# Four-layer attention and feed-forward stack on one core: rounding, dequantising and values moved from VectorE to GpSimd, with a new order table

## Chip, core and metric

The kernel runs on one core of a Trainium2 chip. The metric is the device time of one execution in microseconds (us). A core has five engines that each work through their own list of instructions in order and meet only at semaphores: TensorE (PE in the rows, its weight loads apart as PEld), VectorE (DVE), ScalarE (ACT), GpSimd (POOL) and SyncE (SP), which here issues nearly all DMAs. Matmul results land in eight PSUM banks, which GpSimd does not read in this kernel.

## What is computed

A batch of 8 sequences of 256 tokens with 256 features passes through four layers. Each layer is a cross-attention with 16 heads of 16 features, followed by a different feed-forward part. The layers are numbered 0 to 3 in the code. What matters here is layer 2 and layer 3:

```python
# layer 2 attention: the values are normed, scaled and shifted (vn_scale, vn_bias)
value = _layernorm(kv @ Wv + bv, vn_scale, vn_bias)
# layer 2 feed-forward ("the wide layer": 256 -> 1024 -> 256)
def _act_quant(x):
    scale = 127.0 / jnp.clip(jnp.max(jnp.abs(x), axis=-1, keepdims=True), 1e-05)
    xq = jnp.clip(jnp.round(x * scale), -128.0, 127.0) / scale
    return x + jax.lax.stop_gradient(xq - x)
gate = jax.nn.silu(_bitlinear(x, w_gate)); up = _bitlinear(x, w_up)
return _bitlinear(gate * up, w_down)
# layer 3 attention: the values are the context itself, no projection
vh = v.reshape(B, S, H, D)
# layer 3 feed-forward: six 256 x 256 matrices of 4-bit numbers, dequantised, plus a low-rank part
w = q.astype(jnp.float32) / 7.5 - 1.0
w = w * jnp.repeat(scale, GROUP, axis=1)
base = jnp.einsum('btd,od->bto', x, w) + bias
lora = jnp.einsum('btr,or->bto', jnp.einsum('btd,rd->btr', x, la), lb)
```

Layers 0 and 1 have ordinary attention with a causal mask, then a sign-weight matmul (layer 0) and a mixture of 16 routed and 2 shared experts (layer 1).

## The kernel before

A batch element is one tile of 256 tokens, held as two row blocks of 128 tokens (`SJ = 2`), so the wide layer has 16 row blocks, numbered `T`. Each attention item `(L, b)` has 16 heads. Scores are computed twice: once for the row maxima (`maxima` on PE, `reduce` on DVE, L2196 in the causal layers and L2200 in the others), once transposed for the exponents (`score` on PE, `exp` on ACT, L1945). `values` multiplies by the values held in `v` (PE, L1637). Two halves of `v` serve successive items in turn: who writes values for an item must wait until the item two places earlier has finished its `values` (the semaphore `pv_done`).

All the work is written as small steps (a method of `Part` on each engine). Steps that belong together form a lane, a Python generator that yields between steps. The order in which the lanes advance is the long table `AT`, one row of numbers per lane: all numbers are sorted and the lane that owns the next number advances by one step. Every engine walks the same sorted list and emits only its own methods, so this table fixes the order of instructions on every engine and also the choice of PSUM banks. The numbers are sort keys, and nothing here reads them as times.

The items run in the order of `ORDER`: layers 0 and 1 interleaved first, then layer 2 with layer 3 four items behind. In the trace, layer 2's first exponents begin near 528 us and the last item, (3, 7), begins its exponents near 1094 us.

Steps of VectorE that the change touches, with their lines in the profile:

- `quantise(b)`: maximum of each row, scales (L2388 to L2396), then for each of two row blocks a multiply and round (L2401), and a subtract, clip and cast to bf16 into `xq` (L2408). PE transposes `xq` next (`quantised`, L1756).
- `hidden_quant(T)`: the same for 1024 features: maximum and scales (L2426 to L2431), round (L2433, 128 x 1024), clip and cast into `hid_q`, a part of `xn_t` (L2437). PE transposes it next (`down_turn`, L1778).
- `value_scale(b)`: multiply the normed values by a vector (L2176), then add one into `v` for each row block (L2181).
- `v_take(3, b)`: for layer 3, copy the context into `v` (L2161, two copies).
- `lora_add(n)`, six times: integers to f32 (L2374), times the group scales (L2378), plus the low-rank product from PSUM (L2381).

GpSimd has the small operations of every layer norm (`power`, L2517 to L2523: two tensor-scalar operations, a power, a multiply; ACT cannot norm before them), the lower parts of the split keys and queries (`split_low`, L2542 and L2544), bias additions (L2595, L2715), routing arithmetic, and indirect DMAs (L2681, L2694).

The lines around the value steps before:

```python
def value_scale(b):
    dve.wait_ge(*ln_done.at(("v", b, SJ - 1)))
    V.tensor_tensor(toks["v"], toks["v"], spread(V_L2VS, SJ), ALU.mult).then_inc(*tok_made.step(b))
    before = same_side_before(2, b)
    dve.wait_ge(*pv_done.at((*before, HG - 1)))
```

## Time and profile before

| | us |
|---|---|
| median of 3 runs | 1198.68 |
| lowest and highest | 1193.59, 1200.58 |
| the profiled execution, whole | 1198.55 |
| its span in the trace | 1196.6 |

The span is what the profile's rows cover, from the first to the last instruction. It is 1.95 us shorter than the profiled execution's own time, and that execution lies 0.13 us below the median. Busy times are sums over an engine's instructions. An engine's share of a stretch is its busy time divided by the length of the stretch. Matmul ends are modelled, so PE's share is to be read against other stretches of the same trace and not against 100%.

### The profile page before, as it was taken

The page shows a single profiled execution, that of the slowest core. Times are in us where ns is not written, and L with a number is a line of the kernel's source. Part 1 is how long each engine was busy: PE and PEld are TensorE (multiplying, and loading weights), DVE is VectorE, ACT ScalarE, POOL GpSimd, SP SyncE. Part 2 cuts the span into 40 slices and gives each one's busy share as a digit, 9 for nine tenths or more (in the row PEclk, how much of TensorE's full clock was granted, in tenths as well). Part 3 has the DMA queues.
Part 4 walks back from the last instruction along what each step waited for, and adds up shares of the span by engine and source line. Part 5 has one row for each costly group of instructions (what it writes and reads, how often), then busy time and mean ns, then how long its engine had stood idle before and what let it go on. Part 6 is the DMA issues. An engine that isn't in the chain of part 4 may idle for free.

```text
span 1196.6 us, 26279 instructions
## 1 busy us (share of the span) xinstructions
PE 1067.9 (89%) x8350; PEld 796.2 (67%) x8406; DVE 945.9 (79%) x3207; ACT 826.6 (69%) x1560; POOL 488.3 (41%) x1027
## 2 busy tenths in 40 slices
PE   6998999999999988899999988798899999988876
PEld 4676777777887765666677765366576766656654
DVE  3898888878555788877967798999999989898732
ACT  5777666657665666365667667457889798979953
POOL 6233356653122457657601144233334433423334
PEclk9999999999999999888999998999999999999988
DMA  7885332226777245303587752222203212121000
GB/s 221 260 275 180 87 101 71 85 76 189 218 211 213 89 121 140 85 14 116 150 259 229 233 167 80 56 69 82 82 19 87 72 54 81 53 63 54 10 10 18
DMA packets 102326, 140.03 MB, mean 117 GB/s; under 512 B 12336, under 2 KB 79792, under 8 KB 102192
## 3 DMA queue, kind: packets, MB, share of 16 engines
q1 hardware_dynamic: 99120, 129.97, 37.3%
q0 software_dynamic: 3072, 8.39, 2.2%
q8 instruction: 70, 1.15, 0.4%
q14 instruction: 64, 0.52, 0.1%
HBM read 65.43 MB, written 22.54 MB: 74 GB/s over the span
## 4 chain that ended last, share of the span: by engine, by line
PE 48%; DVE 20%; ACT 11%; DMA 7%; issue 6%; POOL 4%; SPq 3%; another core or an unknown queue 0%; DVEq 0%; ACTq 0%; POOLq 0%
PE ps L1516 10%; PE ps L1637 5%; PE ps L1536 4%; PE ps L1554 4%; PE ps L1729 4%; PE ps L1509 3%; DVE neg_max L2200 3%; PE ps L1523 3%; DVE ps L2196 3%; ACT probs L1945 3%; PE ps L1696 2%; DMA w<-in_expert 2%; ACT q_st L1960 2%; PE ps L1736 2%; DVE bn L2077 2%
## 5 line engine op out<-in xcount | busy, mean ns | idle before, releaser
L1945 ACT ACTIVATE probs<-ps 128x384 f32<-128x384 f32 (+1 forms) x512 | 263.5, 543 | 68.0 <-PE ps L1557 32.3
L1536 PE MATMUL ps<-k_st,q_st 96*128 96x256 bf16 (+1 forms) x1024 | 178.8, 265 | 19.4 <-DVE neg_max L2196 9.7
L1554 PE MATMUL ps<-q_st,k_st 104*128 104x256 bf16 (+1 forms) x1024 | 179.2, 263 | 14.8 <-ACT q_st L1960 6.7
L2200 DVE TENSOR_REDUCE neg_max<-ps 128x2 f32<-128x512 f32 x256 | 168.0, 679 | 11.7 <-PE ps L1536 4.9
L1960 ACT ACTIVATE q_st<-ps 8x1024 bf16<-8x1024 f32 x128 | 130.1, 1016 | 42.3 <-PE ps L1619 39.4
L2517 POOL TENSOR_SCALAR var_eps<-mv 128x2 f32<-128x2 f32 (+1 forms) x115 | 29.0, 252 | 298.0 <-DVE mv L2080 286.9
L2196 DVE CUSTOM_DVE_ANT_0 ps<-ps,diag_s 128x128 f32<-128x128 f32 (+1 forms) x384 | 123.3, 357 | 24.1 <-PE ps L1536 23.4
L1536 PEld LDWEIGHTS ps<-k_st,q_st 96*128 96x128 bf16 x1024 | 88.4, 100 | 70.3 <-DVE neg_max L2196 17.5
L1554 PEld LDWEIGHTS ps<-q_st,k_st 104*128 104x128 bf16 x1024 | 90.9, 99 | 60.3 <-issue 16.3
L1637 PE MATMUL ps<-probs,v 128*32 128x256 f32 (+1 forms) x2048 | 123.0, 359 | 4.7 <-ACT probs L1945 2.8
L2542 POOL CAST parts<-qf 128x512 bf16<-128x512 f32 x64 | 39.1, 612 | 205.2 <-DVE qf L2094 101.9
L1637 PEld LDWEIGHTS ps<-probs,v 128*32 128x32 f32 x2048 | 54.6, 109 | 51.4 <-issue 27.9
L2520 POOL TENSOR_TENSOR rstd<-var_eps,neg_half 128x2 f32<-128x2 f32 (+1 forms) x115 | 83.9, 729 | 0.0
L1953 ACT ACTIVATE o_raw<-ps 128x256 f32<-128x256 f32 x128 | 48.9, 382 | 46.7 <-PE ps L1637 39.2
L2544 POOL TENSOR_TENSOR parts<-qf,parts 128x512 bf16<-128x512 f32 x64 | 75.0, 1172 | 5.2
L1896 ACT ACTIVATE xn<-x,shift,rstd 128x256 f32<-128x256 f32 x112 | 63.8, 630 | 16.6 <-POOL shift L2523 12.0
L1516 PE MATMUL ps<-w,xn_t 128*128 128x256 f32 x296 | 71.2, 383 | 1.6 <-ACT xn_t L1853 1.4
L2196 DVE DVE_READ_ACCUMULATOR2_ANT neg_max<- 128x1 f32 x512 | 71.9, 140 | 0.0
L1729 PE MATMUL ps<-ring,w 128*128 128x128 f32 x496 | 66.9, 279 | 5.5 <-DMA w<-in_expert 4.8
L1557 PE MATMUL ps<-diag_t,ident_b 128*128 128x256 bf16 x256 | 70.6, 276 | 0.0
L1729 PEld LDWEIGHTS ps<-ring,w 128*128 128x128 f32 x496 | 61.4, 191 | 11.0 <-issue 7.9
L1516 PE MATMUL ps<-w,ctx_t 128*128 128x256 f32 x256 | 61.2, 382 | 2.2 <-DVE qf L2102 1.5
(270 smaller groups left out, 2545.8 us busy)
## 6 DMA issues: line engine op xcount, KB each, us to landing
k_st<-parts SPq DMA_DIRECT2D x192, 128.0 KB
q_st<-parts SPq DMA_DIRECT2D x192, 128.0 KB
w<-in_expert SPq DMA_DIRECT2D x62, 384.0 KB, 3.9
x_rows<-wo SPq DMA_DIRECT2D x10, 768.0 KB, 7.1
ctx_t<-in_ctx_t SPq DMA_DIRECT2D x16, 256.0 KB, 3.0
ring<-x_rows SPq DMA_DIRECT2D x31, 128.0 KB, 3.9
y_rows<-ring SPq DMA_DIRECT2D x31, 128.0 KB, 3.8
xn_t<-x_rows SPq DMA_DIRECT2D x31, 128.0 KB, 3.4
```

The source lines that it names most:

```text
L1516: last = mm(t[:, a * D:(a + 1) * D], act_t[:, kt, a * P:(a + 1) * P], weight[:, kt, :], start=kt == 0, stop=kt == KT - 1)
L1536: last = mm(t[:, c0:c0 + n], head(q_st, r, h, KROWS, j * P, P), head(k_st, r, h, KROWS, 0, n), start=j == 0 or L != 2, stop=L != 2, skip_g ...
L1554: last = mm(t[:, j * S:j * S + n], head(k_st, r, h, KALL, j * P, P), head(q_st, r, h, KALL, skip, n), start=j == 0 or L == 3, stop=L == 3, ...
L1557: last = mm(t.rearrange("p (j t) -> p j t", j=SJ)[:, :, 0:P], ident_b[:, :], diag_t[:, L, :, :], start=False, stop=True, skip_group_check= ...
L1637: last = mm(t[h4 * DPAD:(h4 + 1) * DPAD, skip:S], v[:, r, j, hg * HPG + h4, :], probs[:, (hg % 2) * HPG + h4, j * S:(j + 1) * S - skip], s ...
L1729: last = mm(t[:, n * P:(n + 1) * P], expert[:, i % RING, c0:c0 + INNER_E], x_tile_t[:, i % 2, kt * P:(kt + 1) * P], start=kt == 0, stop=kt ...
L1945: nc.scalar.activation(probs[:, (hg % 2) * HPG + h4, 0:width], tile_of(key)[:, 0:width], ACT.Exp, scale=SCALE).then_inc(*tile_drained(key))
L1960: nc.scalar.activation(out, tile_of(key)[KROWS:KALL, 0:S].unsqueeze(1).to_broadcast([2 * HPG, HPG, S]), ACT.Copy).then_inc(*tile_drained(key))
L2196: last = V.tensor_tensor_reduce(some, some, diag_s[:, n0:n0 + j * step + 1:step, :], -1.0, -NEG, ALU.add, ALU.min, neg_max[:, hg, h4, j:j ...
L2200: V.tensor_reduce(neg_max[:, hg, h4, :], tile_of(key).rearrange("p (j t) -> p j t", j=SJ), AX.X, ALU.max, negate=True).then_inc(*tile_drai ...
L2520: G.tensor_tensor(rstd[:, kind, tiles], var_eps[:, kind, tiles], neg_half[:, 0:SJ if a is None else 1], ALU.pow).then_inc(*ln_rstd.step((p ...
L2544: G.tensor_tensor(parts[:, 2, n, :, :], rest, parts[:, 1, n, :, :], ALU.subtract).then_inc(*part_lo.step((what, L, b)))
```

## The change

GpSimd takes over five things from VectorE. Three get a step of their own in their lane: `quantise_round` after `quantise`, `hidden_round` after `hidden_quant`, and `lora_scale` before `lora_add`. The other two move whole: `value_scale`, and the copy of the context for layer 3, now `v_copy`. The operations keep their operands and types; the semaphores between them are renamed (`xq_round`, `hid_round`, `lora_made`). The maxima and scales, and the addition of the low-rank product from PSUM, stay on VectorE. The values of layers 0 and 1 stay there too.

```diff
@@ between loads of the low-rank part and its sum
         part.lora(n)
         yield
+        part.lora_scale(n)
+        yield
         part.lora_add(n)
@@ wide layer
     part.quantise(b)
     yield
+    part.quantise_round(b)
+    yield
     part.quantised(b)
...
     part.hidden_quant(T)
     yield
+    part.hidden_round(T)
+    yield
     part.down_turn(T)
@@ values of layer 3
-    part.v_take(3, b)
+    part.v_copy(3, b)
@@ new on GpSimd (taken out of VectorE's quantise, hidden_quant, lora_add, v_take, value_scale)
+                def value_scale(b):
+                    pool.wait_ge(*ln_done.at(("v", b, SJ - 1)))
+                    G.tensor_tensor(toks["v"], toks["v"], spread(V_L2VS, SJ), ALU.mult).then_inc(*tok_made.step(b))
+                    before = same_side_before(2, b)
+                    pool.wait_ge(*pv_done.at((*before, HG - 1)))
+                    pool.wait_ge(*tok_made.at(b))
+                    for a in range(SJ):
+                        G.tensor_tensor(v[:, side(2, b), a, :, 0:DH], toks["v"][:, a, :].rearrange("p (h d) -> p h d", d=DH),
+                                        vec[:, V_L2VB, :].rearrange("p (h d) -> p h d", d=DH), ALU.add).then_inc(
+                            *v_ready.step((2, b, a)))
+                def v_copy(L, b):
+                    pool.wait_ge(*pv_done.at((*same_side_before(L, b), HG - 1)))
+                    r = side(L, b)
+                    pool.wait_ge(*ctxn_in[b % 4].at(b))
+                    for a in range(SJ):
+                        G.tensor_copy(v[:, r, a, :, 0:DH], h_of(b)[:, a, :].rearrange("p (h d) -> p h d", d=DH)).then_inc(
+                            *v_ready.step((L, b, a)))
+                def lora_scale(n):
...
+                    G.tensor_scalar(w3[:, n, :, :], w3[:, n, :, :].bitcast(I32), 1.0 / 7.5, -1.0, ALU.mult, ALU.add).then_inc(
...
+                    G.tensor_tensor(w3[:, n, :, :], w3[:, n, :, :], scale3, ALU.mult).then_inc(*lora_made.step(("mul", n)))
+                def quantise_round(b):
+                    pool.wait_ge(*quant.at(("dq_hid", b)))
...
+                        G.tensor_scalar(flat[:, a, :], flat[:, a, :], qscale[:, T:T + 1], ROUND, ALU.mult, ALU.add).then_inc(
...
+                        wait_filled(pool, ("xq", b - 1))
...
+                        G.tensor_scalar(xq[:, a, :], flat[:, a, :], ROUND, Q_MAX, ALU.subtract, ALU.min).then_inc(
...
+                def hidden_round(T):
+                    pool.wait_ge(*quant.at(("dqd", T)))
+                    G.tensor_scalar(h, h, hscale[:, T:T + 1], ROUND, ALU.mult, ALU.add).then_inc(*hid_round.step(T))
...
+                        wait_filled(pool, ("ht", T - SJ))
+                    G.tensor_scalar(hid_q[:, a, :], h, ROUND, Q_MAX, ALU.subtract, ALU.min).then_inc(*hid_ready.step(T))
@@ SyncE, before the loads of the 4-bit matrices
-                    wait_filled(sp, ("gd", NTILE - 1))
+                    for i in range(NTILE - RING, NTILE):
+                        wait_filled(sp, ("gd", i))
@@ order table, a row of it
-    (45, 240, 245, 249, 255, 260, 265, 770),
+    (47, 58, 63, 223, 267, 272, 277, 687),
...
```

The wait for the low-rank matrices also moves from batch element 0 to whichever element comes first for each of the three blocks. Every row of the table is new, so the order changes on all engines from the start of the program, also in the layers whose work is the same.

VectorE, in the wide layer at row block T = 9, before: L2426 to L2431 find the maximum and scales of `hid` (in `ring`), L2433 and L2437 round. `before` is the tensor that holds the scales.

```order
L2426 TENSOR_REDUCE before<-ring 128x1 [waits drained3,drained4]
L2428 TENSOR_SCALAR before<-before 128x1 [waits quant]
L2430 RECIPROCAL before<-before 128x1 [waits quant]
L2431 TENSOR_SCALAR before<-before,w_unit 128x1
L2433 TENSOR_SCALAR ring<-ring,before 128x1024 [waits quant]
L2437 TENSOR_SCALAR xn_t<-ring 128x1024 [waits filled3,quant]
L2084 TENSOR_TENSOR ring<-ps,vec 128x512 [waits filled4,filled5]
L2077 BN_STATS bn<-ring 128x6 [waits drained4]
L2077 BN_STATS bn<-ring 128x6
L2080 BN_AGGR mv<-bn 128x2 [waits ln_stats] x2
L2200 TENSOR_REDUCE neg_max<-ps 128x2 [waits filled3]
```

VectorE at the same row block in the changed kernel; L2406 to L2411 are the maximum and scales:

```order
L2406 TENSOR_REDUCE before<-ring 128x1 [waits drained2,drained4]
L2408 TENSOR_SCALAR before<-before 128x1 [waits quant]
L2410 RECIPROCAL before<-before 128x1 [waits quant]
L2411 TENSOR_SCALAR before<-before,w_unit 128x1
L2221 RECIPROCAL sum_inv<-ps 128x8 [waits filled6,filled4]
L2224 TENSOR_TENSOR o_tok<-ps,sum_inv 128x2x64 [waits inverted]
L2197 TENSOR_REDUCE neg_max<-ps 128x2 [waits filled3]
L2197 TENSOR_REDUCE neg_max<-ps 128x2 [waits filled2]
L2197 TENSOR_REDUCE neg_max<-ps 128x2 [waits filled3]
L2197 TENSOR_REDUCE neg_max<-ps 128x2 [waits filled2]
L2208 CAST max_parts<-neg_max 128x2x4 [waits drained2,filled6]
L2210 TENSOR_TENSOR max_parts<-neg_max,max_parts 128x2x4 [waits max_hi]
```

The two 1024-wide roundings are gone from the list, and attention work for other items (L2221, L2224, L2197) follows directly on the scales.

GpSimd at this point before: the split of a query (L2542, L2544), the small operations of two layer norms (L2517 to L2523), and a bias (L2715):

```order
L2542 CAST parts<-qf 128x512 [waits drained6]
L2544 TENSOR_TENSOR parts<-qf,parts 128x512 [waits part_mid]
L2517 TENSOR_SCALAR var_eps<-mv 128x2 [waits ln_moments]
L2518 TENSOR_SCALAR neg_mean<-mv 128x2
L2520 TENSOR_TENSOR rstd<-var_eps,neg_half 128x2 [waits ln_var]
L2523 TENSOR_TENSOR shift<-neg_mean,rstd 128x2 [waits ln_mean,ln_rstd]
L2517 TENSOR_SCALAR var_eps<-mv 128x2 [waits ln_moments]
L2518 TENSOR_SCALAR neg_mean<-mv 128x2
L2520 TENSOR_TENSOR rstd<-var_eps,neg_half 128x2 [waits ln_var]
L2523 TENSOR_TENSOR shift<-neg_mean,rstd 128x2 [waits ln_mean,ln_rstd]
L2715 TENSOR_TENSOR ctx_n<-ctx_n,vec 128x512 [waits drained7]
```

GpSimd in the changed kernel: the same kinds of step in another order (L2570 is the second half of the split, L2491 to L2497 the layer norms, L2741 the bias), with the rounding of T = 9 (L2554, L2558):

```order
L2570 TENSOR_TENSOR parts<-qf,parts 128x512 [waits part_mid]
L2491 TENSOR_SCALAR var_eps<-mv 128x2 [waits ln_moments]
L2492 TENSOR_SCALAR neg_mean<-mv 128x2
L2494 TENSOR_TENSOR rstd<-var_eps,neg_half 128x2 [waits ln_var]
L2497 TENSOR_TENSOR shift<-neg_mean,rstd 128x2 [waits ln_mean,ln_rstd]
L2491 TENSOR_SCALAR var_eps<-mv 128x2 [waits ln_moments]
L2492 TENSOR_SCALAR neg_mean<-mv 128x2
L2494 TENSOR_TENSOR rstd<-var_eps,neg_half 128x2 [waits ln_var]
L2497 TENSOR_TENSOR shift<-neg_mean,rstd 128x2 [waits ln_mean,ln_rstd]
L2554 TENSOR_SCALAR ring<-ring,before 128x1024 [waits quant]
L2558 TENSOR_SCALAR xn_t<-ring 128x1024 [waits filled5,hid_round]
L2741 TENSOR_TENSOR ctx_n<-ctx_n,vec 128x512 [waits drained6]
```

The rounding stands behind two layer norms and in front of the bias. Its second instruction waits for `hid_round`, the signal of the first.

VectorE at the values of layer 2, batch element 5, before: `value_scale` is L2176 and L2181, among row maxima:

```order
L2200 TENSOR_REDUCE neg_max<-ps 128x2 [waits filled3]
L2200 TENSOR_REDUCE neg_max<-ps 128x2 [waits filled2]
L2176 TENSOR_TENSOR w<-w,vec 128x512 [waits ln_done]
L2181 TENSOR_TENSOR v<-w,vec 128x16x16 [waits tok_made,pv_done]
L2181 TENSOR_TENSOR v<-w,vec 128x16x16
L2200 TENSOR_REDUCE neg_max<-ps 128x2 [waits filled3]
L2200 TENSOR_REDUCE neg_max<-ps 128x2 [waits filled2]
L2211 CAST max_parts<-neg_max 128x2x4 [waits drained2,filled7]
L2213 TENSOR_TENSOR max_parts<-neg_max,max_parts 128x2x4 [waits max_hi]
```

GpSimd in the changed kernel, where `value_scale` of the same element is L2510 and L2515:

```order
L2568 CAST parts<-qf 128x512 [waits part_rest]
L2570 TENSOR_TENSOR parts<-qf,parts 128x512 [waits part_mid]
L2510 TENSOR_TENSOR w<-w,vec 128x512 [waits ln_done]
L2515 TENSOR_TENSOR v<-w,vec 128x16x16 [waits tok_made,pv_done]
L2515 TENSOR_TENSOR v<-w,vec 128x16x16
L2491 TENSOR_SCALAR var_eps<-mv 128x2 [waits ln_moments]
L2492 TENSOR_SCALAR neg_mean<-mv 128x2
L2494 TENSOR_TENSOR rstd<-var_eps,neg_half 128x2 [waits ln_var]
L2497 TENSOR_TENSOR shift<-neg_mean,rstd 128x2 [waits ln_mean,ln_rstd]
L2491 TENSOR_SCALAR var_eps<-mv 128x2 [waits ln_moments]
L2492 TENSOR_SCALAR neg_mean<-mv 128x2
L2494 TENSOR_TENSOR rstd<-var_eps,neg_half 128x2 [waits ln_var]
```

The wait for `pv_done` now stands in GpSimd's list, ahead of the small operations of two layer norms.

## Rows read from the trace of the kernel before

**Rows 1.** The page's chain of work that ended last, by engine.

```profile
PE 48%; DVE 20%; ACT 11%; DMA 7%; issue 6%; POOL 4%; SPq 3%; another core or an unknown queue 0%; DVEq 0%; ACTq 0%; POOLq 0%
```

**Rows 2.** Busy time by stretch: start:end, length, engines (instructions), clock, DMA, GB/s.

```profile
0.00:400.00 400.00, 370.06 (x3180) 298.45 (x3181) 297.07 (x1418) 259.75 (x541) 162.70 (x370) 0.99 0.56 168
400.00:560.00 160.00, 140.62 (x1077) 106.72 (x1080) 132.01 (x514) 92.66 (x183) 102.64 (x222) 0.94 0.34 96
560.00:700.00 140.00, 133.71 (x1005) 102.67 (x1020) 107.09 (x279) 90.33 (x201) 34.77 (x79) 1.00 0.68 199
700.00:900.00 200.00, 169.59 (x1240) 113.34 (x1255) 183.71 (x432) 142.26 (x237) 76.36 (x137) 0.95 0.27 77
900.00:1100.00 200.00, 180.37 (x1408) 122.42 (x1424) 181.13 (x450) 177.59 (x291) 76.11 (x144) 0.99 0.25 67
1100.00:1197.00 97.00, 73.54 (x450) 52.63 (x450) 44.88 (x118) 63.99 (x110) 35.67 (x77) 0.91 0.03 12
```

**Rows 3.** The same view, for two stretches of 100 us.

```profile
800.00:900.00 100.00, 89.24 (x675) 62.36 (x683) 93.52 (x221) 80.46 (x133) 36.38 (x71) 0.98 0.21 59
900.00:1000.00 100.00, 93.64 (x697) 64.40 (x708) 90.55 (x228) 90.34 (x150) 40.22 (x76) 0.98 0.23 62
```

**Rows 4.** Groups by form on VectorE: count | busy us, mean ns | idle before, releaser.

```profile
L2433 DVE TENSOR_SCALAR ring<-ring,before 128x1024 f32<-128x1024 f32 x16 | 13.3, 830 | 0.6
...
L2437 DVE TENSOR_SCALAR xn_t<-ring 128x1024 bf16<-128x1024 f32 x16 | 12.1, 755 | 0.6
...
L2176 DVE TENSOR_TENSOR w<-w,vec 128x512 f32<-128x512 f32 x8 | 6.5, 813 | 0.0
L2181 DVE TENSOR_TENSOR v<-w,vec 128x256 f32<-128x256 f32 x16 | 6.2, 423 | 2.6 <-PE ps L1637 1.9
...
L2408 DVE TENSOR_SCALAR xn_t<-xn 128x256 bf16<-128x256 f32 x16 | 5.0, 353 | 0.0
L2401 DVE TENSOR_SCALAR xn<-xn,before 128x256 f32<-128x256 f32 x16 | 4.9, 350 | 0.3
...
L2378 DVE TENSOR_TENSOR w<-w,mask_raw 128x512 f32<-128x512 f32 x6 | 4.2, 692 | 0.2
...
L2161 DVE COPY v<-ctx_n 128x256 f32<-128x256 f32 x12 | 3.6, 338 | 0.0
...
L2374 DVE TENSOR_SCALAR w<-w 128x512 f32<-128x512 int32 x6 | 3.1, 518 | 0.0
```

**Rows 5.** VectorE's L2433 by stretch: start:end, length, busy (count), clock, DMA, GB/s.

```profile
700.00:900.00 200.00, 5.04 (x6) 0.95 0.27 77
900.00:1100.00 200.00, 5.18 (x6) 0.99 0.25 67
```

**Rows 6.** Groups by form on GpSimd, columns as in group 4.

```profile
L2542 POOL CAST parts<-qf 128x512 bf16<-128x512 f32 x64 | 39.1, 612 | 205.2 <-DVE qf L2094 101.9 <-DVE qf L2102 61.1 <-DVE qf L2100 41.9
...
L2517 POOL TENSOR_SCALAR var_eps<-mv 128x2 f32<-128x2 f32 x109 | 27.6, 253 | 290.5 <-DVE mv L2080 286.9
...
L2715 POOL TENSOR_TENSOR ctx_n<-ctx_n,vec 128x512 f32<-128x512 f32 x18 | 22.8, 1273 | 23.4 <-ACT xn_t L1853 23.4
...
L2706 POOL TENSOR_TENSOR mask_raw<-mask_raw,vec 128x256 f32<-128x256 f32 x6 | 4.3, 728 | 7.8 <-ACT xn_t L1853 6.4 <-ACT xn_t L2052 1.4
```

**Rows 7.** PE and GpSimd waits, 700 to 1100 us: total, times, longest.

```profile
PE ps L1756 <- DVE xn_t L2408: 5.9, 4, 3.2
...
POOL var_eps L2517 <- DVE mv L2080: 134.7, 37, 12.3
```

**Rows 8.** Timeline: start us, length us, engine, line; one free, one beside GpSimd.

```profile
993.37 0.75 DVE L2433 TENSOR_SCALAR ring<-ring,before 128x1024 f32<-128x1024 f32 x1
...
1006.05 1.27 POOL L2715 TENSOR_TENSOR ctx_n<-ctx_n,vec 128x512 f32<-128x512 f32 x1 [3.31 <-ACT xn_t L1853]
1006.46 1.41 DVE L2433 TENSOR_SCALAR ring<-ring,before 128x1024 f32<-128x1024 f32 x1
```

**Rows 9.** VectorE's L2094: shortest/median/longest ns, first and last start.

```profile
L2094 DVE TENSOR_TENSOR qf<-qf,parts x16: 658/681/748, 475.3 to 968.3; 128x512 f32<-128x512 f32 x16
```

97 lines of the change are left out of this document (40 added, 57 removed), and 1062 rows, old and new, of the table AT.

## The prediction, made before the changed kernel ran

> **What bounds the kernel now.** I read the page's chain first, then busy time by stretch, then the groups and waits of the stretches where VectorE is fullest. The chain has no single owner: PE 48%, VectorE 20%, ScalarE 11% [rows 1]. So an edit on VectorE can pay only in stretches where VectorE is what the others wait for. The stretches show where that may be [rows 2]. Up to 400 us PE is busy for 370.06 of 400 us (92.5%) and VectorE for 297.07 (74%). From 560 to 700 us PE is at 133.71 of 140 (95.5%, the highest share in this table) and VectorE at 107.09 (76%). From 700 to 900 us it turns round: VectorE 183.71 of 200 (91.9%), PE 169.59 (84.8%), ScalarE 142.26 (71%), at a granted clock of 0.95. From 900 to 1100 us all three are high: PE 180.37, VectorE 181.13, ScalarE 177.59 of 200. The last 97 us are a tail in which no engine is full: PE 73.54, VectorE 44.88. GpSimd is busy for 76 of 200 us in both long stretches, and much of its idle time there is waiting for VectorE: 134.7 us before the first operation of a layer norm [rows 7]. VectorE is therefore the first limit from 700 to 900 us, one of three from 900 to 1100 us, and PE is the limit before 700 us.
>
> **What leaves VectorE.** The groups give it directly [rows 4]: rounding of 1024 features 13.3 + 12.1, rounding of 256 features 4.9 + 5.0, scaling of values 6.5 + 6.2, the two steps of dequantising 3.1 + 4.2. The context copy shows twelve of its sixteen instructions, 3.6 us; the other four read another tensor, and at the same 0.3 us add 1.2, so 4.8. Together 60.1 us of VectorE's 945.9 (the sum of its column in [rows 2] is 945.9). Where they lie: six of the sixteen 1024-wide roundings stand between 700 and 900 us and six between 900 and 1100 us [rows 5], so four stand before 700. The other per-element steps go with them. All but dequantising is 52.8 us, so 6/16 of it, 19.8 us, lies in each of the two long stretches and 13.2 before 700 us. The 7.3 us of dequantising I put at 700 to 900 us, before the layer 3 feed-forward that needs it, which makes 27.1 us there.
>
> **From 700 to 900 us.** VectorE goes from 183.7 to 156.6 us. It has been at 93.5% of a stretch [rows 3], and at that density 156.6 us fit into 167.5. PE is late next. Its 169.6 us need 177.6 us at its best share of 95.5%, and 181.2 us at 93.6%, the share it reaches from 900 to 1000 us, where the mix of work is nearest to this one [rows 3]. I take the latter: 200 − 181.2 = **19 us gained**. Bounds: nothing, if the share of PE stays; and 31 us, if the clock also comes back from 0.95 to 1.00, because PE's 169.6 us are then 161.1, and 161.1/0.955 is 168.7.
>
> **From 900 to 1100 us.** VectorE goes from 181.1 to 161.3 us and is free. PE's 180.4 at 93.6% need 192.7 us. ScalarE's 177.6 us would then stand at 92.2%, a little above the 90.3% of its fullest stretch [rows 3], at which it needs 196.7. I take PE's value, **7 us gained**; bounds 0 and 11 (PE at 95.5%: 188.9).
>
> **Before 700 us.** The 13.2 us that leave VectorE are hidden by PE, which is at 95.5% from 560 to 700 us. Only a few lie before 560 us, where PE has 87.9% and VectorE 82.5%. I take **1 us**; bounds 0 and 3. The first 400 us contain no edit at all, only the new order. PE at 95.5% there would be 387.5 us, 12.5 us less; the row after it (400 to 560 us, 87.9%) shows that an order can also leave PE emptier, and at two points less than now (90.5%) it would be 409 us, 9 us more. With both signs open I take 0.
>
> **What GpSimd gets.** A cast of 128 x 512 takes 612 ns and a one-input operation of two elements 253, a slope of 0.70 ns for each element. Two-input operations take 1273 ns for 512 elements and 728 for 256, a slope of 2.13 [rows 6]. The 1024-wide roundings have one tensor input: 253 + 1024 x 0.70 = 970 ns by the first slope, 1273 + 512 x 2.13 = 2364 by the second. I take the first, since the operand count is the same. For 256 elements that is 432 ns, up to 728. The sum: 32 x 0.97 + 32 x 0.43 + 6 x (0.61 + 1.27) + 8 x (1.27 + 2 x 0.73) + 16 x 0.43 = 31.0 + 13.8 + 11.3 + 21.8 + 6.9 = 85 us, at worst about 145. GpSimd's busy time, 488 us as the sum of its column in [rows 2], becomes 573, and in the stretch from 700 to 900 us 76 becomes about 115 of 200. As throughput this is free; the idle time hides it. As latency it isn't: a rounded row block is ready 2 x 0.97 = 1.94 us after its scales instead of 0.83 + 0.76 = 1.59, plus one more hand-over between engines. PE already waits for the rounded rows, 5.9 us in four waits [rows 7]. In the new lists attention work stands right behind the scales on VectorE, so it covers what PE waits for in most places. I take **1 us lost**.
>
> **Both engines on one port.** A rounding of 1024 takes 0.75 us with GpSimd idle and 1.41 us when GpSimd's 1.27 us addition began 0.41 us earlier [rows 8]. The excess, 0.66, is near the 0.86 that the addition had still to run. The mean of 830 ns against 0.75 us [rows 4, 8] is that effect, and it leaves VectorE with the rounding. What stays and reads two tensors is at 681 ns in the median and 748 at most [rows 9], so such delays were rare there. GpSimd is busier now; I take **1 us lost** for all of these, bounds 0 and 12.
> The Trainium skill states the mechanism in "SBUF — State Buffer", section "Who interferes with whom": VectorE in a two-port mode or with two SBUF inputs and GpSimd take a shared pair of ports for a whole instruction, and the second one waits. By this rule, the trace agrees in rows 8, and the some 70 such instructions that stay on VectorE would each risk part of a GpSimd instruction: at one in four and 0.6 us, 11 us instead of 1, and the end result would be 1183.5.
> The Trainium skill also speaks against the change in "GPSIMD Engine Reference", section "4.1 Engine selection": elementwise work belongs on VectorE, GpSimd being about twice as slow with two inputs. The trace agrees (1273 ns against 692 for 512 elements in rows 4 and 6), but it would change the sum only if GpSimd were short of time.
>
> **The sum.** −19 − 7 − 1 + 1 + 1 = −25 us. Span 1196.6 − 25 = 1171.6; with the 1.95 us around the span the forecast is **1173.5**. The profiled execution (1198.55) stands 0.13 below the median, so the same number serves for the median.
>
> **Rivals.**
> *A, PE bounds it anyway.* PE's 92.5 to 95.5% in two of the three stretches up to 700 us speak for it, and its 48% of the chain. VectorE's idle time then grows by what was removed. Against it speaks the drop of PE to 84.8% exactly where VectorE is at 91.9%. If PE's share from 700 to 1100 us rises by one point only, from 87.5 to 88.5%, its 350.0 us need 395.5 instead of 400; less the 2 us of cost that is −2.5: about 1196.
> *B, the new order pays as well.* If the first 400 us also rise to 95.5% of PE and the clock returns from 700 to 900 us, it is −12.5 − 31 − 11 − 3 + 2 = −55: about 1143. I see no reason in the rows for the first 400 us; half of this, 1157, is the likelier form.
> *C, GpSimd's list becomes the thing waited for: slower.* The sixteen waits for `pv_done` now stand in GpSimd's list, in front of layer norms that ScalarE needs. On VectorE they cost 2.6 us [rows 4]. Eight batch elements each pass two 1024-wide roundings, one 256-wide, one scaling and one copy, 40 steps that take 85 − 11 = 74 us on GpSimd. If each holds a layer norm or a split behind it for its own length, 1.85 us, and that is on the chain, it is 74 us. From one step in three on (25 us) it eats the whole gain. With half of them it is 37 − 27 = +10: about 1209. For it: ACT and PE wait for results of GpSimd's small operations, and its list is in order. Against it: GpSimd keeps 85 of 200 us idle, and the table was rewritten with the new steps in it, spread among the others.
> *D, the change doesn't do what it says.* The lists show the instructions gone from VectorE, so I give this nothing.
>
> **Chances.** Forecast 0.50 (its own range 1160 to 1188), A 0.18, B 0.15, C 0.17. The forecast's range follows from 0 to 31, 0 to 11 and 0 to 12 for its terms, not all at an end at once. To hold 8 in 10, the range reaches down to B's likelier form and up over A: **1152 to 1197**. What this measurement can tell from no change is about 0.5%, 6 us: the borders are 1192.7 and 1204.7. Faster by more: the forecast, B and a part of A, 0.72. Within: most of A and the mild end of C, 0.14. Slower: the rest of C, 0.14.
>
> **What the changed profile would show.** VectorE's busy time near 886 us; GpSimd's near 573. The 1024-wide roundings on GpSimd at 0.97 us each; at 2 us or more the slope was wrong. PE's share in the stretch from 700 to 900 us above 90% with a clock of 0.98 or more; if it stays near 85%, A or C holds. The first 400 us of the trace before compared by the start of the same items: equal within 5 us, or the order is a term of its own. Under C, ScalarE's waits for GpSimd's `shift` and GpSimd's waits for PE's L1637 come up from nearly nothing to tens of us. The forecast fails most simply if PE's share is set by its own list, for then the freed VectorE time is just idle.

## The result, and the profile after

The changed kernel takes 1219.86 us (median of 4 runs, 1214.81 to 1223.59) against 1199.47 us for the kernel before: a ratio of 1.0177, with a 95% interval of 1.0125 to 1.0229. It is slower by about 21 us, where 25 us less were forecast. The time lies outside the range (1152 to 1197). The profiled execution took 1221.66 us, its span is 1219.9.

First the page of the changed kernel: busy time by engine, then the chain that ended last, by engine.

```profile
PE 1080.7 (89%) x8350; PEld 798.2 (65%) x8406; DVE 899.3 (74%) x3091; ACT 819.2 (67%) x1556; POOL 628.8 (52%) x1143
...
PE 42%; DVE 15%; POOL 14%; issue 10%; ACT 8%; DMA 6%; SPq 5%; another core or an unknown queue 0%; DVEq 0%; ACTq 0%; POOLq 0%
```

VectorE is down from 945.9 to 899.3 us, most of the way to the 886 foreseen. GpSimd is at 628.8 and not at 573, and its share of the chain has gone from 4% [rows 1] to 14%. Four of the stretches of [rows 2], with the same columns (stretch, length, then PE, PEld, DVE, ACT and POOL busy, granted clock, DMA share, GB/s):

```profile
0.00:400.00 400.00, 370.63 (x3129) 296.31 (x3129) 288.77 (x1395) 257.08 (x535) 162.61 (x370) 0.98 0.56 168
...
560.00:700.00 140.00, 126.43 (x935) 97.59 (x951) 93.54 (x255) 86.10 (x191) 60.52 (x106) 0.99 0.68 200
700.00:900.00 200.00, 173.16 (x1216) 114.43 (x1236) 163.32 (x382) 135.15 (x230) 139.74 (x183) 0.92 0.29 85
900.00:1100.00 200.00, 173.96 (x1321) 116.06 (x1336) 159.23 (x379) 164.42 (x270) 108.86 (x162) 0.96 0.21 59
```

The first 400 us are as before (370.63 against 370.06 of PE). From 700 to 1100 us VectorE has its idle time, as planned: 163 and 159 of 200 instead of 184 and 181. But PE is at 87%, not at the 93.6% assumed, and GpSimd has risen to 139.7 of 200 where about 115 were expected. GpSimd's groups by form say why (count | busy us, mean ns | idle before, releaser; all of these rows are new on GpSimd):

```profile
L2558 POOL TENSOR_SCALAR xn_t<-ring 128x1024 bf16<-128x1024 f32 x16 | 58.5, 3657 | 1.3
...
L2554 POOL TENSOR_SCALAR ring<-ring,before 128x1024 f32<-128x1024 f32 x16 | 18.0, 1123 | 67.6 <-DVE before L2411 67.5
L2547 POOL TENSOR_SCALAR xn_t<-xn 128x256 bf16<-128x256 f32 x16 | 17.9, 1117 | 1.3
...
L2515 POOL TENSOR_TENSOR v<-w,vec 128x256 f32<-128x256 f32 x16 | 12.2, 784 | 4.2 <-PE ps L1653 3.4
L2510 POOL TENSOR_TENSOR w<-w,vec 128x512 f32<-128x512 f32 x8 | 10.6, 1323 | 0.1
...
L2533 POOL TENSOR_TENSOR w<-w,mask_raw 128x512 f32<-128x512 f32 x6 | 7.6, 1268 | 3.1 <-DMA mask_raw<-in_lb 2.7
L2540 POOL TENSOR_SCALAR xn<-xn,before 128x256 f32<-128x256 f32 x16 | 7.5, 482 | 4.6 <-DVE before L2387 4.4
```

The two halves of a rounding, which took the same time on VectorE (830 and 755 ns, [rows 4]), take 1123 and 3657 ns on GpSimd, though both read one tensor of 128 x 1024 and write one. The multiply-and-add (L2554) is near the price assumed, 970 ns. The subtract-and-minimum (L2558) costs 3.8 times that, and more than the upper bound of 2364. At 256 features it is 482 against 1117 ns. The value steps came as priced.

Who waits for it, from 560 us on (total us, times, longest):

```profile
POOL ring L2554 <- DVE before L2411: 67.5, 12, 31.5
...
PE ps L1794 <- POOL xn_t L2558: 16.9, 8, 3.0
...
PE ps L1772 <- POOL xn_t L2547: 9.1, 5, 3.1
...
POOL v L2524 <- PE ps L1653: 8.2, 1, 8.2
```

L1794 and L1772 are the transposes `down_turn` and `quantised` (L1778 and L1756 before). PE waits 26.0 us for the clipped rows. In the same stretch before it was 6.8 us: the 5.9 us of [rows 7] and 0.9 us in front of L1778. One such place in the timeline (start us, length us, engine, line; in square brackets the idle time before and what ended it):

```profile
713.80 1.12 POOL L2554 TENSOR_SCALAR ring<-ring,before 128x1024 f32<-128x1024 f32 x1 [6.11 <-DVE before L2411]
...
715.00 3.63 POOL L2558 TENSOR_SCALAR xn_t<-ring 128x1024 bf16<-128x1024 f32 x1
...
718.78 1.01 PE L1794 MATMUL ps<-ident_b,xn_t 128*128 128x128 bf16 x8 [3.00 <-POOL xn_t L2558]
...
719.83 1.02 ACT L2043 ACTIVATE xn_t<-ps 128x1024 bf16<-128x1024 bf16 x1 [2.82 <-PE ps L1794]
...
720.25 0.69 DVE L2197 TENSOR_REDUCE neg_max<-ps 128x2 f32<-128x512 f32 x1 [3.33 <-PE ps L1550]
```

The attention work put between the scales and the transpose covers about the first 2 us of GpSimd's work; then PE stands still for 3.0 us, and with it ScalarE and VectorE, which wait for PE.

### The profile page after: what moved, and what is told of

It reads as the page before. It is cut to its first block, busy times and chain, and to the rows that moved or that the text cites. A ratio compares the mean times of both kernels' runs of the same rounds, so it can differ in the third digit from the quotient of the medians.

```text
span 1219.9 us, 26288 instructions
## 1 busy us (share of the span) xinstructions
PE 1080.7 (89%) x8350; PEld 798.2 (65%) x8406; DVE 899.3 (74%) x3091; ACT 819.2 (67%) x1556; POOL 628.8 (52%) x1143
## 4 chain that ended last, share of the span: by engine, by line
PE 42%; DVE 15%; POOL 14%; issue 10%; ACT 8%; DMA 6%; SPq 5%; another core or an unknown queue 0%; DVEq 0%; ACTq 0%; POOLq 0%
PE ps L1530 9%; PE ps L1523 5%; PE ps L1550 4%; PE ps L1653 4%; POOL xn_t L2558 4%; PE ps L1568 4%; SPq L2788 3%; DVE ps L2193 3%; PE ps L1537 2%; PE ps L1745 2%; DMA w<-in_expert 2%; ACT probs L1962 2%; DVE neg_max L2197 2%; PE ps L1712 2%; PE ps L1571 2%
## 5 line engine op out<-in xcount | busy, mean ns | idle before, releaser
L1962 ACT ACTIVATE probs<-ps 128x384 f32<-128x384 f32 (+1 forms) x512 | 260.7, 544 | 85.7 <-PE ps L1571 28.4
L1550 PE MATMUL ps<-k_st,q_st 96*128 96x256 bf16 (+1 forms) x1024 | 175.0, 265 | 26.4 <-DVE neg_max L2193 9.2
L2197 DVE TENSOR_REDUCE neg_max<-ps 128x2 f32<-128x512 f32 x256 | 169.0, 680 | 38.4 <-PE ps L1550 18.1
L1653 PE MATMUL ps<-probs,v 128*32 128x256 f32 (+1 forms) x2048 | 126.4, 366 | 0.8 <-POOL v L2524 0.3
L2491 POOL TENSOR_SCALAR var_eps<-mv 128x2 f32<-128x2 f32 (+1 forms) x115 | 27.1, 236 | 182.7 <-DVE mv L2094 176.1
L2570 POOL TENSOR_TENSOR parts<-qf,parts 128x512 bf16<-128x512 f32 x64 | 75.0, 1172 | 5.2
L1530 PE MATMUL ps<-w,ctx_t 128*128 128x256 f32 x256 | 64.3, 398 | 0.3 <-DVE ring L2398 0.3
```

The costliest lines, as they stand in the source:

```text
L1530: last = mm(t[:, a * D:(a + 1) * D], act_t[:, kt, a * P:(a + 1) * P], weight[:, kt, :], start=kt == 0, stop=kt == KT - 1)
L1550: last = mm(t[:, c0:c0 + n], head(q_st, r, h, KROWS, j * P, P), head(k_st, r, h, KROWS, 0, n), start=j == 0 or L != 2, stop=L != 2, skip_g ...
L1653: last = mm(t[h4 * DPAD:(h4 + 1) * DPAD, skip:S], v[:, r, j, hg * HPG + h4, :], probs[:, (hg % 2) * HPG + h4, j * S:(j + 1) * S - skip], s ...
L1962: nc.scalar.activation(probs[:, (hg % 2) * HPG + h4, 0:width], tile_of(key)[:, 0:width], ACT.Exp, scale=SCALE).then_inc(*tile_drained(key))
L2197: V.tensor_reduce(neg_max[:, hg, h4, :], tile_of(key).rearrange("p (j t) -> p j t", j=SJ), AX.X, ALU.max, negate=True).then_inc(*tile_drai ...
L2570: G.tensor_tensor(parts[:, 2, n, :, :], rest, parts[:, 1, n, :, :], ALU.subtract).then_inc(*part_lo.step((what, L, b)))
```

## The experiments

Two explanations were open. Either the long second half loses the time, or the new order table does, with the steps moved for nothing. Each ratio below is to the kernel before, run on the same chip at the same time, with its 95% interval. That kernel's own median differed between the three sets of runs (1193.10, 1196.24 and 1198.73 us), so kernels are compared by their ratios and not by their times. A change of 0.01 is 12 us. The changed kernel's 1.0177 comes from the first comparison, of four runs each, and is known to about 0.005.

**All five steps back on VectorE, the new table kept.** The functions `value_scale`, `v_copy`, `lora_scale`, `quantise_round` and `hidden_round` stand in VectorE's part again, at the places that the new table gives them.

```diff
@@ the five functions, moved from GpSimd's part to VectorE's; one of them
-                    pool.wait_ge(*quant.at(("dqd", T)))
-                    G.tensor_scalar(h, h, hscale[:, T:T + 1], ROUND, ALU.mult, ALU.add).then_inc(*hid_round.step(T))
+                    dve.wait_ge(*quant.at(("dqd", T)))
+                    V.tensor_scalar(h, h, hscale[:, T:T + 1], ROUND, ALU.mult, ALU.add).then_inc(*hid_round.step(T))
```

> The changed kernel with all five steps back on VectorE, so the new order table alone. Theory S: the changed kernel loses because the clip-and-cast of the rounding takes 3.64 us for 1024 features and 1.12 us for 256 on GpSimd (0.69 and 0.28 to 0.35 us on VectorE); then this kernel is near the one before, 1195 to 1205 us. Rival O, the new order is the cause whatever engine does the work: it stays at 1215 to 1222 us, and (2,0) to the end is as long as in the changed kernel.

Measured: 1206.43 us, ratio 1.0093 [1.0061, 1.0124]. That is between the ranges of the two theories. The table without the move (with the few waits that were changed along with it) costs 11 us. That is about half of the whole loss, and it was taken as nothing. What grew most is the waiting of PE's score matmuls for VectorE's row maxima, from 560 us on. Of this kernel (its maxima are L2249):

```profile
PEld ps L1550 <- DVE neg_max L2249: 40.7, 57, 2.4
...
PE ps L1550 <- DVE neg_max L2249: 21.8, 34, 2.0
```

and of the kernel before, in the same stretch:

```profile
PEld ps L1536 <- DVE neg_max L2200: 11.5, 27, 1.1
...
PE ps L1536 <- DVE neg_max L2200: 3.6, 9, 0.8
```

The matmuls' wait has gone from 3.6 to 21.8 us, that of the weight loads (PEld) from 11.5 to 40.7; the two can overlap in time. The likely reading is that the new order counts on a VectorE that is free for the maxima, and with the roundings back in its list it is not. No run isolates this, and such waits are not lost time one for one: the fastest kernel below, with the same table and the roundings on GpSimd, has 11.3 and 24.2 us of them, more than the kernel before.

**Only the second halves back on VectorE.** The multiply-and-round stays on GpSimd.

```diff
@@ quantise_round and hidden_round, last instruction; its waits go with it
-                        G.tensor_scalar(xq[:, a, :], flat[:, a, :], ROUND, Q_MAX, ALU.subtract, ALU.min).then_inc(
+                        V.tensor_scalar(xq[:, a, :], flat[:, a, :], ROUND, Q_MAX, ALU.subtract, ALU.min).then_inc(
...
-                    G.tensor_scalar(hid_q[:, a, :], h, ROUND, Q_MAX, ALU.subtract, ALU.min).then_inc(*hid_ready.step(T))
+                    V.tensor_scalar(hid_q[:, a, :], hid[a], ROUND, Q_MAX, ALU.subtract, ALU.min).then_inc(*hid_ready.step(T))
```

> The changed kernel with only the second half of each rounding (subtract, clip, cast to bf16) back on VectorE; multiply-and-round, dequantising and values stay on GpSimd. Theory S: GpSimd loses 76 us of busy time, and the time falls to 1185 to 1198 us, below the kernel before. Rival G, GpSimd's list with its waits for TensorE and its two-input operations is what delays: 1210 us or more.

Measured: 1195.49 us, 1.0017 [0.9988, 1.0045]. Level with the kernel before and 1.6% under the changed kernel. The second halves on GpSimd lose 19 us against the same instructions on VectorE.

**What makes the second half slow: its output type or its arithmetic.** Subtract and minimum stay in f32, and a copy makes the bf16; at 256 features (not shown) it is a single subtraction, without the minimum.

```diff
-                    G.tensor_scalar(hid_q[:, a, :], h, ROUND, Q_MAX, ALU.subtract, ALU.min).then_inc(*hid_ready.step(T))
+                    G.tensor_scalar(h, h, ROUND, Q_MAX, ALU.subtract, ALU.min).then_inc(*hid_round.step((T, "clip")))
+                    pool.wait_ge(*hid_round.at((T, "clip")))
+                    G.tensor_copy(hid_q[:, a, :], h).then_inc(*hid_ready.step(T))
```

> The changed kernel, the 1024-wide clip written as f32 in place and then cast to bf16 by a copy, all on GpSimd; the 256-wide one as a single subtract with bf16 output, which leaves out the upper clip at 127 (the scale puts the largest value there). It tells what makes the clip-and-cast slow. If the bf16 output of a tensor-scalar instruction is slow: the f32 clip takes 1.1 us, the copy 1.0 to 1.2, the single subtract stays near 1.1 us, and the time falls by 10 to 20 us. If the pair subtract and min is slow: the f32 clip stays at 3.6 us, the single subtract falls to 0.45 us, and the time rises above 1220 us.

Measured: 1228.96 us, 1.0271 [1.0216, 1.0326]. GpSimd's groups in this kernel:

```profile
L2558 POOL TENSOR_SCALAR ring<-ring 128x1024 f32<-128x1024 f32 x16 | 58.5, 3656 | 1.3
...
L2560 POOL CAST xn_t<-ring 128x1024 bf16<-128x1024 f32 x16 | 16.6, 1041 | 1.1
L2547 POOL TENSOR_SCALAR xn_t<-xn 128x256 bf16<-128x256 f32 x16 | 13.5, 855 | 0.0
```

The f32 form takes 3656 ns against 3657 with bf16: the type doesn't matter, the arithmetic does. The pure cast of 1024 is 1041 ns, so the slope of [rows 6] was right for a cast. A single subtract at 256 features still takes 855 ns, where 450 were expected if the pair was to blame.

**An addition in place of the subtraction.** At 1024 features one addition of −ROUND and nothing else, at 256 an addition and the minimum. The minimum is the upper clip at 127. The scale puts the largest value of a row at 127, so it never acts, and this kernel and the following ones can leave it out.

```diff
-                        G.tensor_scalar(xq[:, a, :], flat[:, a, :], ROUND, Q_MAX, ALU.subtract, ALU.min).then_inc(
+                        G.tensor_scalar(xq[:, a, :], flat[:, a, :], -ROUND, Q_MAX, ALU.add, ALU.min).then_inc(
...
-                    G.tensor_scalar(hid_q[:, a, :], h, ROUND, Q_MAX, ALU.subtract, ALU.min).then_inc(*hid_ready.step(T))
+                    G.tensor_scalar(hid_q[:, a, :], h, -ROUND, None, ALU.add).then_inc(*hid_ready.step(T))
```

> The changed kernel with other forms of the second half of the roundings, all on GpSimd with bf16 output. 1024-wide: one addition of the negated constant (the upper clip is left out; the scale puts the largest value at 127). 256-wide: addition and min. If subtract is the slow operation: 1.1 us for 1024 and 0.5 us for 256. If min is slow as well: 1.1 us for 1024, and 0.75 to 1.1 us for 256. If every tensor-scalar instruction that isn't multiply and add is slow: about 2.5 us (253 ns plus 1024 times the 2.35 ns of the single subtract).

Measured: 1205.07 us in one run, beside 1196.24 for before. The same two groups:

```profile
L2558 POOL TENSOR_SCALAR xn_t<-ring 128x1024 bf16<-128x1024 f32 x16 | 45.0, 2811 | 1.3
...
L2547 POOL TENSOR_SCALAR xn_t<-xn 128x256 bf16<-128x256 f32 x16 | 18.1, 1129 | 1.3
```

Even a single addition takes 2811 ns for 1024 elements, 2.5 times the first half, which adds as well but multiplies first. So it is not the subtraction, and not the minimum alone. The second operation has a share in the slow forms (855 ns for one at 256 features, 1117 and 1129 for two), but the first half has two operations as well and is fast.

**Multiply by one, then add −ROUND.** The pair of the first half, used for the second, again without the minimum. Below it is called the fast form.

```diff
-                        G.tensor_scalar(xq[:, a, :], flat[:, a, :], ROUND, Q_MAX, ALU.subtract, ALU.min).then_inc(
+                        G.tensor_scalar(xq[:, a, :], flat[:, a, :], 1.0, -ROUND, ALU.mult, ALU.add).then_inc(
...
-                    G.tensor_scalar(hid_q[:, a, :], h, ROUND, Q_MAX, ALU.subtract, ALU.min).then_inc(*hid_ready.step(T))
+                    G.tensor_scalar(hid_q[:, a, :], h, 1.0, -ROUND, ALU.mult, ALU.add).then_inc(*hid_ready.step(T))
```

> The changed kernel with the second half of both roundings written as multiply by one and add the negated constant, on GpSimd (the upper clip is left out; it never acts). The form is that of the first half, so 1.1 to 1.2 us for 1024 and 0.5 us for 256, 50 us less of GpSimd's time. Theory S, the length of these instructions is the whole loss beyond the table's: 1185 to 1197 us, at or below the kernel with them on VectorE (1195.5). Rival G, the extra hand-over and GpSimd's list cost as well: 1200 to 1212 us.

Measured: 1182.61 us (five runs, 1180.35 to 1185.71), 0.989 [0.9855, 0.9926]. This beats the kernel before by 1.1% and the changed one by 2.8%, and is a little better than the 1185 to 1197 us expected. Its groups, then its busy time and chain, and its two long stretches:

```profile
L2558 POOL TENSOR_SCALAR xn_t<-ring 128x1024 bf16<-128x1024 f32 x16 | 17.1, 1068 | 1.3
...
L2547 POOL TENSOR_SCALAR xn_t<-xn 128x256 bf16<-128x256 f32 x16 | 6.7, 432 | 0.0
```

```profile
PE 1072.0 (91%) x8406; PEld 791.7 (67%) x8406; DVE 898.7 (76%) x3091; ACT 818.5 (69%) x1556; POOL 577.0 (49%) x1143
...
PE 45%; DVE 19%; ACT 10%; issue 7%; POOL 7%; DMA 6%; SPq 5%; DVEq 0%; ACTq 0%; POOLq 0%
```

```profile
700.00:900.00 200.00, 178.53 (x1342) 118.73 (x1339) 172.70 (x410) 150.45 (x253) 124.59 (x201) 0.96 0.32 92
900.00:1100.00 200.00, 183.97 (x1452) 122.92 (x1453) 172.59 (x415) 178.00 (x292) 95.48 (x172) 1.00 0.21 58
```

The durations are those of the prediction (970 and 432 assumed, 1068 and 432 measured), and so is GpSimd's busy time (573, 577.0). PE is up at 89% and 92%.

**Other orders and pairs.** Add then multiply by one at 1024, multiply then subtract at 256.

```diff
-                        G.tensor_scalar(xq[:, a, :], flat[:, a, :], ROUND, Q_MAX, ALU.subtract, ALU.min).then_inc(
+                        G.tensor_scalar(xq[:, a, :], flat[:, a, :], 1.0, ROUND, ALU.mult, ALU.subtract).then_inc(
...
-                    G.tensor_scalar(hid_q[:, a, :], h, ROUND, Q_MAX, ALU.subtract, ALU.min).then_inc(*hid_ready.step(T))
+                    G.tensor_scalar(hid_q[:, a, :], h, -ROUND, 1.0, ALU.add, ALU.mult).then_inc(*hid_ready.step(T))
```

> The changed kernel with two more forms of the second half, bf16 output on GpSimd (upper clip left out): 1024-wide as add, then multiply by one; 256-wide as multiply by one, then subtract. If only the pair multiply-then-add is fast: 2.8 us or more for 1024, and 0.85 to 1.1 us for 256. If any pair of add, subtract and multiply is fast: 1.1 and 0.45 us.

Measured: 1192.86 us in one run, beside 1198.73.

```profile
L2547 POOL TENSOR_SCALAR xn_t<-xn 128x256 bf16<-128x256 f32 x16 | 17.3, 1092 | 0.0
L2558 POOL TENSOR_SCALAR xn_t<-ring 128x1024 bf16<-128x1024 f32 x16 | 17.0, 1064 | 1.3
```

Multiply and add are fast in either order (the second order was run at 1024 features only). A multiply with a subtract, run at 256 only, is about as slow as subtract with minimum (1092 and 1117 ns).

**The table of before, with the steps on GpSimd.** Two kernels: once with the slow second half as in the change, once with multiply-and-add. Each new step stands directly behind the maxima and scales, since the old rows have no place for it of its own.

```diff
@@ the order table of before; in its lanes, for example
     part.hidden_quant(T)
+    part.hidden_round(T)
     yield
     part.down_turn(T)
```

> All five steps on GpSimd as in the changed kernel, but with the order table of before; each moved step stands in GpSimd's list at the place of the VectorE step it follows. Theory S: this order gives the slow roundings no room, so it is slower than the changed kernel, 1225 to 1260 us. Rival O: with the old order the loss is gone, 1195 us or less.

Measured: 1259.05 us, 1.0542 [1.0477, 1.0606]. And with the fast form:

> All five steps on GpSimd in the multiply-and-add form (the upper clip is left out), with the order table of before. If only the length of the instructions counted, it is at or below 1193 us, as the old order alone is 13 us better than the new one. If their places in the lists count, since the old table has each moved step directly in front of what waits for it, 1205 to 1230 us.

Measured: 1213.56 us, 1.0155 [1.0113, 1.0198]. With the kernel before and the changed one they make a table of ratios:

| | steps on VectorE | steps on GpSimd, fast form | steps on GpSimd, as changed |
|---|---|---|---|
| table of before | 1 | 1.0155 | 1.0542 |
| new table | 1.0093 | 0.989 | 1.0177 |

With the fast form, either part alone loses and together they gain. The new table is worth 2.6% to the moved steps (0.989 against 1.0155), 3.5% in the slow form, and costs 0.9% without them. One difference is that the new table has a place of its own for each new step, so other work can stand between a rounding and the transpose that needs it. With the old table PE waits, from 560 us on, 12.9 us for rounded rows even in the fast form, and ScalarE waits 33.3 us for `shift`, the last of GpSimd's small results of a layer norm, against 20.1 us in the kernel before.

**The values back on VectorE**, in the kernel with the fast form: `value_scale` and `v_copy` in VectorE's part.

```diff
@@ value_scale and v_copy, moved from GpSimd's part to VectorE's; in them
-                    pool.wait_ge(*pv_done.at((*before, HG - 1)))
+                    dve.wait_ge(*pv_done.at((*before, HG - 1)))
```

> The multiply-and-add version with the two value steps back on VectorE; roundings and dequantising stay on GpSimd. VectorE gets 17.5 us back. If VectorE's time is worth something there, it is 3 to 8 us slower than the version with the values on GpSimd. If the waits for TensorE in GpSimd's list cost (the rival of the prediction), it is faster by 3 us or more. Equal within 2 us: the values are hidden on either engine.

Measured: 1186.08 us (nine runs), 0.992 [0.9889, 0.9952], the same as 0.989 within the intervals. So the move of the values, with its waits for `pv_done` in GpSimd's list (the place of rival C), makes no difference that can be seen. A small cost and a small gain that cancel would look the same.

**Which slow form does the harm.** The fast form at one width, the slow one at the other. First slow at 256 only:

```diff
@@ against the kernel with multiply and add at both widths
-                        G.tensor_scalar(xq[:, a, :], flat[:, a, :], 1.0, -ROUND, ALU.mult, ALU.add).then_inc(
+                        G.tensor_scalar(xq[:, a, :], flat[:, a, :], ROUND, Q_MAX, ALU.subtract, ALU.min).then_inc(
```

> The multiply-and-add version with the slow form (subtract and min, 1.12 us instead of 0.43) on the 256-wide roundings only, 11 us more of GpSimd's time. If each microsecond of these instructions counts alike, it is 8 us slower than the multiply-and-add version: about 1191 us. If the wide layer's first step is nearest to the chain: 10 to 20 us slower. If it is hidden: within 3 us.

Measured: 1193.88 us, 0.9942 [0.9911, 0.9973]. Then slow at 1024 only:

```diff
@@ against the kernel with multiply and add at both widths
-                    G.tensor_scalar(hid_q[:, a, :], h, 1.0, -ROUND, ALU.mult, ALU.add).then_inc(*hid_ready.step(T))
+                    G.tensor_scalar(hid_q[:, a, :], h, ROUND, Q_MAX, ALU.subtract, ALU.min).then_inc(*hid_ready.step(T))
```

> The multiply-and-add version with the slow form (3.66 us instead of 1.07) on the 1024-wide roundings only, 41 us more of GpSimd's time. Of the 37 us between the changed kernel and the multiply-and-add version this is to hold 25 to 35: 1208 to 1218 us.

Measured: 1211.39 us, 1.0075 [1.0044, 1.0107]. Over the fast form that is 0.5% (6 us) and 1.9% (22 us). The 6 us are weak, since the interval of that ratio just overlaps the fast form's. Together it is 2.4%, and the changed kernel is 2.9% over the fast form. The slow seconds are 16 x 2.59 = 41 us at 1024 and 16 x 0.69 = 11 us at 256: a little over half of what GpSimd spends more arrives at the end in both.

**Late results, or a list held up.** A long instruction does two things: its own result comes later, and everything behind it in GpSimd's list comes later. Here the rounded rows are signalled on time and then unneeded work stands in the list, of which nobody reads the result: three powers and an addition on `pad`, a small tensor of ones.

```diff
@@ hidden_round, against the kernel with multiply and add at both widths
                     G.tensor_scalar(hid_q[:, a, :], h, 1.0, -ROUND, ALU.mult, ALU.add).then_inc(*hid_ready.step(T))
+                    if T:
+                        pool.wait_ge(*hid_round.at(("pad", T - 1)))
+                    else:
+                        pool.wait_ge(*const_ready.at("pad"))
+                    for i in range(1, 4):
+                        G.tensor_tensor(pad[:, 2 * i:2 * i + 2], pad[:, 0:2], neg_half[:, 0:2], ALU.pow)
+                    G.tensor_scalar(pad[:, 8:10], pad[:, 0:2], 0.0, None, ALU.add).then_inc(*hid_round.step(("pad", T)))
```

> The multiply-and-add version, and behind each 1024-wide rounding, after its result is signalled, about 2.5 us of instructions on GpSimd that nobody needs (three powers and an addition of two elements each). The rounded rows are not late; only GpSimd's list is held for as long as in the slow form. Theory L, the rows' lateness on TensorE is the loss: 1183 to 1188 us. Theory H, what stands behind in GpSimd's list is the loss: 1205 to 1218 us, as with the slow form itself.

Measured: 1201.41 us, 1.001 [0.9975, 1.0046]. The added work, in GpSimd's groups:

```profile
L2566 POOL TENSOR_TENSOR pad<-pad,neg_half 128x2 f32<-128x2 f32 x48 | 33.6, 724 | 0.0
...
L2567 POOL TENSOR_SCALAR pad<-pad 128x2 f32<-128x2 f32 x16 | 4.5, 283 | 0.0
```

That is 3 x 0.724 + 0.283 = 2.46 us at each wide rounding, near the 2.59 of the slow form, and it costs 1.2% (14 us) over the fast form where the slow form costs 1.9% (22 us). The time lies between the ranges of the two theories. Holding the list is enough to lose more than half of that, with no rounded row later than in the fast form (PE waits 0.7 us for the 1024-wide rows in both). What came late is in ScalarE's waits for `shift`, the layer norms, from 560 us on, here

```profile
ACT xn L1914 <- POOL shift L2499: 13.4, 6, 4.8
...
ACT ring L1914 <- POOL shift L2499: 9.5, 8, 2.1
```

and in the kernel with the fast form alone

```profile
ACT xn L1913 <- POOL shift L2497: 10.0, 6, 3.5
...
ACT ring L1913 <- POOL shift L2497: 4.9, 5, 1.4
```

8 us more between them. The kernel with the slow form at 1024 shows its loss elsewhere:

```profile
PE ps L1794 <- POOL xn_t L2558: 17.1, 8, 3.0
...
ACT xn L1913 <- POOL shift L2497: 7.4, 7, 1.5
...
ACT ring L1913 <- POOL shift L2497: 6.2, 6, 1.9
```

PE waits 17.1 us for the rows (0.7 with the fast form), and the layer norms are not later than with it (13.6 against 14.9 us in these two rows). So a held list alone can cost 14 us, but in the slow form it does not show as such: what shows there is the wait on the rows. It may be that the list catches up while PE stands still, but that is not shown. No run has late rows without a held list, so how the slow form's 22 us divide between the two stays open.

## Why the prediction was wrong, point by point

The course of five kernels shows where time went. The marks are the starts (us) of the 257th, 321st, 385th, 449th and 512th exponents on ScalarE, read from the counts of that line to within 1 us; the first is where layer 2 begins.

| | 257th | 321st | 385th | 449th | 512th |
|---|---|---|---|---|---|
| before | 528 | 733 | 883 | 1008 | 1122 |
| new table alone | 529 | 738 | 887 | 1022 | 1135 |
| new table, fast form | 531 | 739 | 878 | 1006 | 1114 |
| as changed | 532 | 750 | 895 | 1036 | 1151 |
| table of before, fast form | 525 | 741 | 900 | 1024 | 1139 |

*The price of a rounding on GpSimd: the step that failed.* The prediction took one slope for all operations with one tensor input, from a cast. The slope holds for casts and for multiply with add (1041, 1123 and 1068 ns at 1024), and fails for subtract with minimum: 3657 against 970, beyond the upper bound of 2364. A rounding takes 4.78 us and not 1.94, so the one microsecond set for latency became 2.9% (0.989 to 1.0177), 34 us. This alone turns the sign. The second halves are 32 of the 64 rounding instructions, and no row of the trace before showed that operation on that engine; the bounds came from rows of other operations, and the upper one was treated as safe. The prediction did name 2 us as the sign that the slope was wrong. The trace before also held a warning on small tensors that was overlooked. These are two of GpSimd's groups in it, both a single minimum, one over 16 elements and one over 32:

```profile
L2663 POOL TENSOR_SCALAR less<-less 128x16 f32<-128x16 f32 x8 | 2.0, 248 | 0.7
...
L2650 POOL TENSOR_SCALAR past<-past 128x32 f32<-128x32 f32 x8 | 2.4, 296 | 0.7
```

48 ns for 16 elements are 3.0 ns for each, four times the slope of the cast. By that a minimum over 1024 would be estimated at 248 + 1008 x 3.0 = 3270 ns.

PE's granted clock was lower in the slower kernel: 0.92 from 700 to 900 us as changed and 0.96 in the fast form (0.95 before), then 0.96 and 1.00 from 900 to 1100 us (0.99 before). How much of the 34 us comes through the clock is not separated.

The Trainium skill says in "GPSIMD Engine Reference", section "4.1 Engine selection", that elementwise work with one input is roughly line-rate on GpSimd. The measurements come near this for casts and for multiply with add (1041 to 1123 ns, beside 755 to 830 on VectorE). Subtract with minimum takes 3.4 times as long as multiply with add, and the measurement decides.

*The order table: a term taken as nothing.* In the first 400 us that was right: PE is busy for 370.6 of 400 as before, and layer 2 begins within 4 us of the old time. It was wrong to look for the table's effect there only. From the 257th exponent on, the new table with unchanged work loses 13 − 1 = 12 us, 10 of them between the 385th and the 449th. The prediction compared engines' totals by stretch and moved steps out of them as if the rest kept its place.

*What leaves VectorE.* 60.1 us foreseen, 46.6 measured. The groups did leave in full. But the busy times of groups overlap in time: before, they sum to 1111.1 us where VectorE is busy for 945.9, and that sum falls by only 51.6, to 1059.5. About 8 us were added by what stays (the small steps on `max_parts` 4.6 us, the two forms of L2108 1.2 and 0.8 us longer in sum), and 5 us of the groups that left had been covered by others. L2108 beside GpSimd:

```profile
763.97 1.16 POOL L2570 TENSOR_TENSOR parts<-qf,parts 128x512 bf16<-128x512 f32 x1
764.23 1.45 DVE L2108 TENSOR_TENSOR qf<-ctx_t,parts 128x512 f32<-128x512 f32 x1
```

Its 16 instructions of the form in [rows 9] are now at (shortest/median/longest):

```profile
L2108 DVE TENSOR_TENSOR qf<-qf,parts x16: 679/682/1404, 489.6 to 985.3; 128x512 f32<-128x512 f32 x16
```

The longest was 748. The median hasn't moved, so long delays stay rare, and 1 us was the right size. By the Trainium skill, "SBUF — State Buffer", section "Who interferes with whom", a VectorE instruction with two SBUF inputs waits out one on GpSimd that has the shared ports, and here the trace agrees: 1.45 us is near the 0.90 us left of L2570 plus 0.68 of its own. The 11 us that this rule could have cost do not show: all that stays on VectorE has grown by 8 us in sum, and L2108 by 2.0 of these.

*From 700 to 1100 us, −19 and −7.* About half of it came, and only once the second half is fast. Against the kernel before, the fast form takes 375 us from the 321st to the 512th exponent instead of 389: 14 us gained where 26 were foreseen, and 13 us (1.1%) over the whole kernel. Against the new table alone it is 1 us behind at the 321st exponent, 9 ahead at the 385th, 16 at the 449th and 21 at the 512th; in ratios that is 0.989 / 1.0093 = 0.980, 24 us. That this is near the 25 forecast is luck, since the forecast was for the change with its table, and with the table of before the same move loses 1.55%. PE's share from 900 to 1100 us came to 92.0%; from 700 to 900 us it was 89.3%, below the 93.6% assumed, and the clock there 0.96. As changed, both stayed at 87%.

*Before 700 us, −1; the latency, +1.* Nothing was gained there even with the fast form. It is 3 us behind the kernel before at the 257th exponent and 6 at the 321st, and 2 and 1 us behind the new table alone. In the fast form PE waits 0.7 us for the 1024-wide rows and 1.9 for the 256-wide, so the latency term was right for the duration that it assumed.

*Rival A* (PE bounds it anyway) is refuted as it was priced: PE's share rises and the kernel gains 1.1% when the second half is fast, though less than forecast. *Rival B* is refuted: the order alone is slower. *Rival C* had the right outcome, a slower kernel through GpSimd's list, but the wrong place. The waits for `pv_done` make 11.6 us of GpSimd's idle time and no difference in the time of the kernel; each step's length does make one, and it had been set at 1.85 us on average where the wide rounding takes 4.8. The sign named for it, ScalarE waiting for `shift`, moved little in the changed kernel (20.1 to 21.4 us over all its lines from 560 us on); PE's wait for `xn_t` moved most. That GpSimd had 60 of 200 us idle from 700 to 900 us did not hide the long steps. Much of its idle time is the wait for scales, which the list has to sit out in order (L2554, 67.5 us from 560 us on).
